# Inverse softmax sums spread over partitions through DRAM instead of by TensorE, V tiles in other banks, a normalisation chain moved to VectorE, and a reordered opening

## What is computed

```
x = x + xattn(layernorm(x), ctx, ctx)      # q from x, k and v from ctx
x = x + ffn(layernorm(x))

q, k = rope(x_ln @ wq.T), rope(ctx @ wk.T);  v = ctx @ wv.T
scores = einsum(q, k) * sqrt(dk), kept where |q - k| <= 128
out = softmax(scores) @ v;  return out @ wo.T + wo_b

hidden = gelu(quant(x) @ quant(W_in) + b_in);  return quant(hidden) @ quant(W_out) + b_out
```

## Time and profile before

| what | value |
|---|---|
| median of 3 runs | 1280.28 us (1279.95 to 1281.63) |
| the profiled execution's own time | 1278.04 us |
| span of its trace | 1276.3 us |
| PE busy | 1154.1 us (90% of the span) |
| DVE busy | 922.8 us (72%) |
| ACT, POOL busy | 641.3 us (50%), 417.6 us (33%) |
| mean granted TensorE clock | 0.979 of full speed |
| first score product of step 0 | 47.52 us |
| steps 1 to 14, each | 44.67 to 46.53 us from first score product to first score product |

### The profile page before, as it was taken

How to read it: one execution, slowest core, us unless ns; L and a number is a source line. 1 busy time by engine, 2 the same in 40 slices (tenths; PEclk the granted TensorE clock), 3 DMA queues, 4 the chain that set the end, 5 groups by cost and what they waited for, 6 DMA issues and landing times.

```text
span 1276.3 us, 23813 instructions
## 1 busy us (share of the span) xinstructions
PE 1154.1 (90%) x7860; PEld 783.8 (61%) x7904; DVE 922.8 (72%) x2362; ACT 641.3 (50%) x999; POOL 417.6 (33%) x768
## 2 busy tenths in 40 slices
PE   4589999999999999999999975999999979999997
PEld 4568777777777877777777753444444434444443
DVE  5568777767877877876786765566666678888885
ACT  5143354354255345335435423655555557777774
POOL 1453465446355346445544521000000012111220
PEclk9799999999999999999999978999999989999999
DMA  7543553563473365355356352255555310577762
GB/s 248 133 107 95 155 133 94 147 161 88 124 187 98 104 171 125 100 150 146 87 141 154 77 156 75 100 197 195 201 203 193 100 49 25 170 227 233 236 206 91
DMA packets 91067, 181.26 MB, mean 142 GB/s; under 512 B 12880, under 2 KB 21328, under 8 KB 90960
## 3 DMA queue, kind: packets, MB, share of 16 engines
q1 hardware_dynamic: 90960, 179.92, 47.9%
HBM read 81.30 MB, written 41.94 MB: 97 GB/s over the span
## 4 chain that ended last, share of the span: by engine, by line
PE 44%; issue 26%; DVE 17%; ACT 5%; POOL 4%; DMA 2%; SPq 1%; POOLq 0%; DVEq 0%; ACTq 0%
PE bank L772 16%; PE bank L564 6%; DVE bank L1037 4%; PE bank L607 4%; PE bank L491 3%; PE bank L492 3%; PE bank L493 3%; PE bank L622 3%; PE bank L580 2%; PE bank L635 2%; DVE bn L999 2%; DVE roped L1063 2%; ACT x_ln L800 2%; PE bank L503 1%; DVE rt L1061 1%
## 5 line engine op out<-in xcount | busy, mean ns | idle before, releaser
L1037 DVE CUSTOM_DVE_ANT_0 bank<-bank,mask 128x256 f32<-128x256 f32 x512 | 201.7, 456 | 89.7 <-PE bank L580 84.0
L772 PE MATMUL bank<-wout_int,g_lo 128*128 128x512 bf16 x512 | 195.5, 382 | 1.3 <-DVE g_lo L1299 0.2
L741 PE MATMUL bank<-qT_lo,win_int 128*128 128x512 bf16 x512 | 194.0, 379 | 2.8 <-DVE qT_lo L1217 1.6
L772 PE MATMUL bank<-wout_int,g_hi 128*128 128x512 bf16 x491 | 187.3, 382 | 9.2 <-DVE g_lo L1299 9.1
L741 PE MATMUL bank<-qT_hi,win_int 128*128 128x512 bf16 x489 | 185.4, 379 | 0.1
L844 ACT ACTIVATE probs<-bank 128x512 f32<-128x512 f32 x256 | 142.5, 603 | 49.4 <-PE bank L607 44.9
L1357 POOL TENSOR_SCALAR_AFFINE_SELECT probs<-probs 128x256 f32<-128x256 f32 x256 | 109.7, 433 | 91.5 <-ACT probs L844 88.7
L1299 DVE TENSOR_TENSOR g_lo<-h_int,g_hi 128x512 f16<-128x512 f32 x128 | 104.3, 815 | 35.9 <-ACT g_hi L966 34.7
L580 PE MATMUL bank<-k_st,q_st 96*128 96x256 f32 x512 | 96.8, 305 | 19.0 <-DMA q_st<-q_lo 11.5
L939 ACT ACTIVATE h_ring<-bank,b_in,g_scale 128x512 f32<-128x512 f32 x96 | 73.6, 779 | 75.4 <-PE bank L741 57.8
L607 PEld LDWEIGHTS bank<-q_st,k_st 128*128 128x128 f32 x512 | 89.4, 189 | 30.3 <-issue 13.2
(11 more groups left out here) (149 smaller groups left out, 2744.7 us busy)
## 6 DMA issues: line engine op xcount, KB each, us to landing
hidden_scratch<-h_ring SPq DMA_DIRECT2D x96, 256.0 KB, 2.0
h_ring<-hidden_scratch SPq DMA_DIRECT2D x96, 256.0 KB, 3.0
k_st<-k_hi SPq DMA_DIRECT2D x128, 128.0 KB, 2.4
q_st<-q_hi SPq DMA_DIRECT2D x128, 128.0 KB, 2.4
xq<-x_scratch SPq DMA_DIRECT2D x16, 1024.0 KB, 6.0
x_ln<-in_x SPq DMA_DIRECT2D x16, 512.0 KB, 4.6
ctx_raw<-in_ctxT SPq DMA_DIRECT2D x16, 512.0 KB, 4.8
k_st<-k_lo SPq DMA_DIRECT2D x64, 128.0 KB, 2.5
```

The costliest lines, as they stand in the source:

```text
L741: mm = pe.matmul(bank[f % 4][:], win_int[:, c, f * P:(f + 1) * P], part[:, par, c], start=c == 0 and part is qT_hi, stop=c == KC - 1 and p ...
L772: mm = pe.matmul(bank[4 * par + u][:], part[:, f % 4, u * P:(u + 1) * P], wout_int[:, f], start=f == 0 and part is g_hi, stop=f == FC - 1 ...
L1037: dve.tensor_tensor_reduce(sc, sc, mask[:, (1 - qb) * P:(1 - qb) * P + S], 1.0, NEG, ALU.add, ALU.max, row_max[:, qb, n:n + 1]).then_inc(m ...
```

## The change

1. **Shares.** The products with `pick` go, with the table. SP writes den_r to DRAM (128 KB), waits until that has landed, and reads it back with each group's four rows repeated for 32 partitions (512 KB) into `share`, which is the memory of the first two `probs` slots. `normalise` reads `share` from SBUF. Both DMAs stand in SP's list in front of the load of x_res.
2. **V tiles** go to `pv_bank` and wait for the copy of the attention output instead of K's rotation. `v_tile(0)` moves up to the third pair. The x transposes move in front of K's second half, and VectorE's `xt_rest` and K rotations each move up by one pair.
3. **First normalisation.** Its 17 operations stand together on VectorE, behind `quantise_win` and in front of the second residual of batch b-1. GpSimd's 14 go; the Newton step has three operations instead of four.
4. **Opening.** wk is loaded, split and used in two halves, with the context between them; the rope table comes before wv; the first stacks are issued leading parts first; VectorE makes Q's rest.

```diff
+            def spread_shares(j):
+
+                sp.wait_ge(den_done, j + 1)
+                sp.dma_start(den_d.rearrange("c (r s) -> (c r) s", s=S), den_r).then_inc(den_out, 16)
+                sp.wait_ge(den_out, 16 * (j + 1))
+                rows = den_d[:, 0:NC4 * S].rearrange("c (o e) -> c o e", o=1).to_broadcast([KC, DK, NC4 * S])
+                sp.dma_start(share, rows).then_inc(share_in, 16)
...
             def step(b, has_o, has_proj, has_xt, has_next):
                 if has_o:
+                    spread_shares(b - 1)
                     load_xres(b - 1)
...
             def normalise(b, half):
-                dve.wait_ge(share_mm, 2 * b + half + 1)
+                dve.wait_ge(oT_out, 2 * b + half + 1)
+                dve.wait_ge(share_in, 16 * (b + 1))
                 part = oT[:, 2 * half:2 * half + 2].rearrange("p i t -> p (i t)")
-                dve.tensor_tensor(part, part, pv_bank[half][:], ALU.mult).then_inc(onorm, 1)
+                dve.tensor_tensor(part, part, share[:, 2 * half * S:2 * (half + 1) * S], ALU.mult).then_inc(onorm, 1)
...
-                    tiles[1] += [lambda: qk_tile(b + 1, "k", 1), lambda: x_transposes(b + 1, 0), lambda: x_transposes(b + 1, 1)]
-                if has_o:
-                    tiles[2] += [lambda: shares(b - 1)]
-                if has_proj:
+                    tiles[1] += [lambda: x_transposes(b + 1, 0), lambda: x_transposes(b + 1, 1), lambda: qk_tile(b + 1, "k", 1)]
+                    tiles[2] += [lambda: v_tile(b + 1, 0)]
                     tiles[3] += [lambda: qk_tile(b + 1, "q", 0)]
                     tiles[4] += [lambda: qk_tile(b + 1, "q", 1)]
-                    tiles[5] += [lambda: v_tile(b + 1, 0)]
-                    tiles[6] += [lambda: v_tile(b + 1, 1, range(2))]
-                    tiles[7] += [lambda: v_tile(b + 1, 1, range(2, KC))]
+                    tiles[5] += [lambda: v_tile(b + 1, 1, range(2))]
+                    tiles[6] += [lambda: v_tile(b + 1, 1, range(2, KC))]
...
-                    between[2] += [lambda: xt_rest(b + 1, 0), lambda: xt_rest(b + 1, 1)]
-                    between[3] += [lambda: rotate(b + 1, "k", 0)]
-                    between[4] += [lambda: rotate(b + 1, "k", 1)]
+                    between[1] += [lambda: xt_rest(b + 1, 0), lambda: xt_rest(b + 1, 1)]
+                    between[2] += [lambda: rotate(b + 1, "k", 0)]
+                    between[3] += [lambda: rotate(b + 1, "k", 1)]
...
                 quantise_win(b)
+                if has_xt:
+                    ln1(b + 2)
                 if has_o:
                     residual(b - 1, 1)
                     ln2_moments(b - 1, 1)
                     largest(b - 1, 0)
-                if has_xt:
-                    ln1_moments(b + 2)
-                if has_o:
                     largest(b - 1, 1)
...
             def step(b, par, has_c, has_o, has_proj, has_xt):
-                if has_proj:
-                    for _ in ln1_scale(b + 1):
-                        pass
                 if has_o:
                     bias_x(b - 1)
```

More of the change, by code:

```diff
@@ L372, in _, with stack_part @@
             load_win(0)
-            sp.wait_ge(w_lo_done, 2)
+            sp.wait_ge(w_lo_done, 3)
             sp.dma_start(weight_stage["wo"], wsrc["wo"]).then_inc(w_in["wo"], 16)
-            sp.wait_ge(w_lo_done, 3)
+            def stack_part(n, i, r, part):
+                sp.dma_start(STACKS[n][DK * r:DK * (r + 1), KC * i:KC * (i + 1)].bitcast(F32),
+                             part[n][DK * i:DK * (i + 1)].bitcast(F32)).then_inc(stacked[n][i], 16)
+            sp.wait_ge(hi_done["k"], 1)
             for i in range(NC4):
-                stack_group("k", 0, i)
+                stack_part("k", i, 0, part_hi)
+                stack_part("k", i, 2, part_hi)
+            sp.wait_ge(lo_done["k"], KC)
             for i in range(NC4):
-                stack_group("q", 0, i)
+                stack_part("k", i, 1, part_lo)
+            sp.wait_ge(hi_done["q"], 1)
+            for i in range(2):
+                stack_part("q", i, 0, part_hi)
+                stack_part("q", i, 1, part_hi)
+            sp.wait_ge(lo_done["q"], KC)
+            for i in range(2):
+                stack_part("q", i, 2, part_lo)
+            for i in range(2, NC4):
+                stack_part("q", i, 0, part_hi)
+                stack_part("q", i, 1, part_hi)
+                stack_part("q", i, 2, part_lo)
             load_ctx(2)
@@ L504, in x_transposes @@
                 mm.then_inc(xt_mm, 1)
[L506 to L513, removed]
-                    mm.then_inc(share_mm, 1)
             def v_tile(j, s, chunks=range(KC)):
-                if chunks[0] == 0:
-                    pe.wait_ge(rope_step["k"], ROPE_OPS * (j + 1))
+                if chunks[0] == 0 and j == 1:
+                    pe.wait_ge(v_done, s + 1)
+                elif chunks[0] == 0:
+                    wait(pe, oT_out, 2 * (j - 2) + s + 1)
                 for c in chunks:
                     tok = slice(s * P, (s + 1) * P)
-                    mm = split3(kv_bank[s][:], (cT_hi[:, c, tok], cT_lo[:, c, tok]),
+                    mm = split3(pv_bank[s][:], (cT_hi[:, c, tok], cT_lo[:, c, tok]),
                                 (w_hi["wv"][:, c], w_lo["wv"][:, c]), c == 0, c == KC - 1)
@@ L582, in scores, with max_transposes @@
                 mm.then_inc(s_mm, 1)
-            def max_transposes(b):
+            def max_transposes(b, has_proj):
                 pe.wait_ge(msplit, 2 * (b + 1))
-                wait(pe, onorm, 2 * b)
+                if has_proj:
+                    pe.wait_ge(v_done, 2 * (b + 2))
+                else:
+                    pe.wait_ge(oT_out, 2 * b)
                 for qb in range(2):
@@ L602, in scores_t @@
                 elif n == 10:
+                    pe.wait_ge(rope_step["k"], ROPE_OPS * (b + 2))
+                elif n == 2 and has_proj:
                     pe.wait_ge(v_done, 2 * (b + 2) - 1)
+                elif n == 2:
+                    pe.wait_ge(oT_out, 2 * b - 1)
                 if before[n] is not None:
@@ L715, in _ @@
             steps(pe, step)
-            shares(NB - 1)
             for _ in o_products(NB - 1, False):
@@ L1001, in moments, with ln1 @@
                 link(dve.bn_aggr(mv[:, which, s], bn[:, which, s]))
-            def ln1_moments(j):
+            def ln1(j):
                 dve.wait_ge(xln_in, 16 * (j + 1))
-                wait(dve, ln1_chain, LN_SC * j)
-                link = chain(dve, ln1_moment, LN_ST * j)
+                link = chain(dve, ln1_chain, LN1_OPS * j)
                 moments(link, x_ln, 0, 0)
@@ L1358, in band @@
                                    pattern=[[0, 2], [1, P]], channel_multiplier=1).then_inc(p_ready, 1)
-            for _ in ln1_scale(0):
-                pass
-            for which, src in (("k", oT), ("q", roped)):
-                for c in range(KC):
-                    split_lo(which, 0, c, src)
+            for c in range(KC):
+                split_lo("k", 0, c, oT)
             for c in range(KC):
```

135 lines of the change are left out of this document (68 added, 67 removed).

## The result

| | before | changed |
|---|---|---|
| median | 1280.12 us (1278.45 to 1281.63) | 1353.44 us (1350.83 to 1353.97) |
| profiled execution, span | 1278.04, 1276.3 us | 1353.58, 1351.9 us |
| mean granted TensorE clock | 0.979 | 0.925 |
| first score product of steps 0, 1, 15 | 47.52, 93.40, 735.18 | 39.88, 86.25, 789.07 |
| from that of step 15 to the end | 541.1 us | 562.8 us |

The ratio is 1.0568, 95% interval [1.0551, 1.0584]: 5.7% slower, where the forecast was 1279 us and its range ended at 1298.

A forecast was written before the change was run, and what follows sets the result against it. TensorE, busy 42.3 of 46 us a step, was taken as the bound, VectorE second. From 1278.0, opening -11, steps -6, step 15 +8 and tail +8 gave 1277 profiled, 1279 us as median; range 1244 to 1298.

The forecast's parts named there:

- the read's price: 512 KB read of the shares on four of sixteen queues: 7.5 us by rate, 8.9 by slope.
- the landing of x_res: Load behind the read lands at t = 18.5 instead of 13.1, t counted in us from the step's start.
- The upper bound: Read of the shares on four of sixteen queues, priced 7.5 us by rate or 8.9 by slope.
- The chain of the first half: After x_res, POOL's bias, K's rest and output's rest, then four output products: transposes at 27.4, 0.45 us less than 27.85.
- The point of no gain: Read landing at t = 17.7, 8.0 us after issue; beyond that each us costs 16.
- Second half: VectorE's ten extra small operations hide in existing waits: 0, up to 1 us a step if ScalarE's normalisation comes late.
- Opening: First product about 3 us sooner, score 0 at about 38.7 instead of 47.52; with step 0's 2 us, -11.
- the 2 us: Step 0 has no shares, and its waits for rotation and rest of x go: 2 us gained.
- Last step and tail: Step 15's transposes at 764.1 against 756.46, +8; behind it the uncovered trip ends at 788.3 against 779.9, +8.
- VectorE's bound of 25.75: VectorE's limit on a step's first half: 27.85 - 0.9 - 1.0 - 0.8 - 0.4 + 1.1 us.
- The fast rival: Read over all sixteen queues lands 3.8 us sooner, steps -2.1 x 14 = -29, median 1249; faster family's chance 0.35.

The follow-up runs named there:

- half of the read: Changed kernel with the narrow read cut to 256 KB, the first half's columns alone, so the second half is not normalised properly; 1286.93 us.
- four reads, loads first, bias late: Changed kernel with the read as four DMAs, issued behind the x_res and x_ln loads, and GpSimd's bias additions behind the output's rest; 1309.41 us.

## Why the prediction was wrong

**The step that failed is the read's price and, with it, the landing of x_res.** The text put the read at 7.5 us, with 8.9 as the upper end, and let x_res follow 1.3 us later, at t = 18.5. Measured were 11.3 us in a step and 9.7 with only x_res beside it, and POOL began on x_res at t = 21.3 in step 6 and 22.2 at the median. The number of engines was right (a DMA share of 0.25 with the read alone), and so was the order: x_res queued behind it and did not interleave. The rate was not. A quarter of 410 GB/s is 102; the read ran at 98 in its first microsecond, but at 76 later, and by the two sizes at 77. While x_res moved on the other twelve engines, a packet of the read took 0.28 to 0.40 us instead of 0.18. The upper bound was therefore no bound: it scaled transfers that nothing disturbed, and had no term for the loads that run beside the read. In a step these are x_res and x_ln, issued 0.7 and 1.1 us after it.

**What it is worth.** The forecast stood at 1277 for the profiled execution, which took 1353.6, so 76.5 us were missed. They are: the first halves of steps 1 to 14, forecast 0.45 us shorter and measured 3.0 longer, 48.4 us; the second halves, 18.6; the last step and the end, 5.6; the opening, 3.9. The chain of the first half was right. It put the transposes 8.9 us behind x_res; they come 8.4 behind it in the changed kernel and 9.0 with half of the read. So the 48.4 us come from x_res, 3.7 us later than t = 18.5 in each step.

**The point of no gain was too late.** By the text the change loses when the read lands after t = 17.7; x_res then lands at 19.0 and the first half is as long as before, 27.85. With half of the read POOL began at 17.7, and the first half was 26.7, as that chain gives, but the step was already 0.3 us longer than before. What is missing there is the second half. From that run to the changed kernel are 4.5 us of landing and 66.5 of time, 14.8 for each, where the text had 16; part of these 14.8 is clock.

**Second half: priced 0, measured +1.3 us a step, 19 us over 14 steps.** The reason given for a possible cost, a late VectorE or ScalarE, is not what happened: at 13.2 and 15.8 the second half is 18.4 with the same VectorE work. It is the clock. Over steps 1 to 14 of eight of the kernels the second half is 18.4 us plus 0.44 us for each microsecond that it spends at 0.50; of the 55 without such time, 52 take 18.3 to 18.4. Before the change no step had any; in the changed kernel each of the 14 has, 1.0 to 4.1 us. A forecast of a wait in front of matmuls should have carried its clock too.

**Opening: -11 forecast, -7.1 measured at step 1.** The first product came at 12.60, as forecast (3 sooner), and the first score at 39.88 against 38.7; the terms of the text add up to 39.1. In step 0 the 2 us did not appear: it took 46.4 us against 45.9. No run took the opening alone; all ten kernels that have it start their scores at 39.8 to 40.8.

**Last step and tail: +8 and +8 forecast, +10.4 and +11.2 measured**, the same undersized read. The clock falls here too: the first output products behind the last step come 0.43 us apart, before the change 0.23.

**VectorE's bound of 25.75** is 25.85 by its own terms. With POOL out of the way the first halves are 25.2, so it held within 0.6 us. One of its terms did not come: normalise was to lose 1.1 us to two operands in SBUF, and takes 0.69 us each as before. The others were not tested one by one. The fast rival, a wide read, was forecast at 1249 with x_res at t = 14.7 and steps 2.1 us shorter. With four wide reads behind the loads its steps came: 1252 us, steps 2.3 us shorter. With the wide reads ahead of the loads, as the rival had it, they did not quite: 1265, x_res at 15.8, steps 1.4 us shorter.

The text also says that the first output product before the change, at 348.92, waits for POOL. Its row shows no idle time: V's products stood in front of it, and that cover is part of what the change took away.

What stays open is the split of the 2.3 us between the shares taken off TensorE and the earlier rotation, and why the four engines moved 76 GB/s even after x_res had left the others.

## What to carry to other kernels

A broadcast through DRAM with 4 pieces outermost ran on a quarter of the engines: write it as several DMAs, here of 32 partitions. Ask first who is issued behind a slow transfer, and put the loads that others wait for ahead of it; here one swap in a list was worth 78 us. An engine's part of a later load stands in line even when most of that load has passed. And count a wait in front of TensorE with the clock that it loses, and an elementwise operation moved on GpSimd together with what VectorE does at that very moment.

## What the hardware showed that was not expected

- A broadcasting read with four outer pieces ran at a DMA share of 0.25: 256 KB in 6.3 us, 512 KB in 9.7, and 11.3 beside other traffic; a load of 512 KB issued behind it took 11.6 instead of 3.7, because its last quarter waited for the read's four engines. As four DMAs of 32 pieces each the read took 2.7 each in the steps, at a share of 1.00 where it ran alone, and 5.2 each when issued behind two loads.
- VectorE's operations of 32 columns, 0.18 us each, took 1.30 and 1.20 beside GpSimd's additions of 1.24: not slowed in proportion, but finished when GpSimd's finished. The row maxima, which take a bank of PSUM, kept their 0.43 to 0.47 us beside GpSimd's subtractions.
- After 4.3 us of idle TensorE (the changed kernel) and 2.5 us (four reads, loads first, bias late) in a stretch at clock 1.00, the clock stood at 0.50, and TensorE ran products for 3.5 and 5.4 us before it was back. On top of the wait itself, the second half lost 0.44 us for each microsecond at 0.50: 18.4 us without, 19.9 with 3.4 us of it.
